# A chunked delta rule: new queue order for the halved chunks, and identity turns on TensorE at the change of state

## The chip, the cores and the metric

One core of one Trainium2 chip runs the whole program. The metric is device time in microseconds (us) of that core, the median of the runs shown.

## The reference, cut to what matters

The program is two layers of attention, scans and experts over x of 4 x 256 x 256. The change lies in one of its eight parts, a gated delta rule with 16 heads of 128 in each of 4 sequences, so 64 lanes of a 128 x 128 state:

```python
def step(S, t):
    q_t, k_t, v_t, a_t, b_t = t
    y = jnp.einsum('bhvk,bhk->bhv', S, k_t)
    err = y - v_t
    S = a_t[..., None] * S - (b_t[..., None] * err)[..., None] * k_t[:, :, None, :]
    o = jnp.einsum('bhvk,bhk->bhv', S, q_t)
    return (S, o)
```

After the scan come a layer norm over each head, a gate sigmoid(x Wg), and the product with Wo.

## The kernel before, in words

The 256 time steps are four blocks of 64. In each block `heads_and_norm` makes q, k, v and the decays a, while the block before is normed and projected. A block has two groups of 32 steps (o = 0 and 1), and a group has four chunks of 8 (jj = 0 to 3; ci = 4 o + jj). At the start of a group the state S of all 64 lanes is turned and multiplied with the keys and queries (`state_t`, `columns`), which gives F, the share of the old state. Between the two groups stands the change of state: the errors W are turned (`turn`), `update` multiplies them with the keys, VectorE adds this to S (`add_update`), and S is turned again for the next group.

Within a chunk VectorE (DVE) runs `chunk`: `key_decays` multiplies the chunk's key products M with decays; `base` puts the starting errors into PSUM; a chunk is solved in two halves of 4 steps, where the second needs products of the first (WH4, turned and multiplied on TensorE in `first_half`, taken in by `carry`). It then writes the errors, lane by lane decayed (WNS, or W in the last chunk), and makes the answers of the queries. TensorE (PE) carries the errors of all chunks so far to the next one: each `hop` turns 128 x 512 errors, ScalarE (ACT) copies them, and 16 small products follow. A chunk jj has jj + 1 hops, and the next chunk's `base` waits for the last of them. POOL (GpSimd) prepares decays for the chunk ahead (`prepare`), and masks the key products (`own_lanes`).

Each engine runs its list of instructions in the order in which the program writes it; the lists meet at semaphores. So the order of the lines is the order of the queues. Beside the chunk's own work, these lists hold `key_rows` (16 keys turned, 16 ACT copies), the decay of the 64 state lanes on ACT (L2589), and in group o = 1 the sixteen `gate` products of the layer's output gate (L2282, 4 per chunk) with their sigmoids.

The list of SP, which starts the transfers, matters too. M is loaded anew for every chunk (`spread`, L1920), into one of two rooms, so chunk ci can be asked for once chunk ci - 2 is finished. The gate's weights WG come four heads at a time (L1946). Both stand in one loop, which the change leaves as it is:

```python
for ci in range(2, NC):
    ...
    spread(n, ci)
    if ci >= NI:
        j = ci - NI
        sp.wait_ge(rest_mm, z["rest_mm"] + NI - 1)
        if j:
            sp.wait_ge(gate_mm, z["gate_mm"] + 4 * j)
        sp.dma_start(WG[:], ...).then_inc(wg_in, 16)
```

`gate_mm` counts finished gate products, `wg_in` the landed weights; `gate(n, h)` waits for load h // 4. `key_decays` of a chunk waits for its M (`m_in`).

Of the kernel before, what the change touches and what calls it, by code (L numbers as in the profile page):

```python
# [1678 lines left out]
def delta_attention(core):  # L1679
# [48 lines left out]
    ZB = sb("ZB", [P, 4 * QU], BF16)  # L1728
    AO = sb("AO", [P, BH])
# [39 lines left out]
    with nc.Block() as block:  # L1769
# [65 lines left out]
        def _(dve):  # L1835
# [24 lines left out]
            "f_d": NO * NS, "ds_d": NO, "dd_d": NC, "mk_d": NC, "mq_d": NC, "fp_d": NC, "wdec_d": NO * (NI - 1), "kt_mm": NO * NR,  # L1860
            "kr_d": NO * NR, "w_d": NC, "base_d": NC, "q_d": NC, "o_d": NC, "wt_mm": NR * NO, "wt_d": NR * NO,
            "kc_d": NO, "ch_mm": NO, "ch_d": NO, "cn_mm": NO, "cn_d": NO, "gh_d": NO, "gn_d": NO * (NI - 1), "wh_d": NC, "ht_mm": NC, "nh_d": NC,
# [21 lines left out]
    MB = flat_df[:, 0:4 * B * NI].rearrange("p (j i b) -> p j i b", j=NI, i=4)  # L1884
    MH = flat_df[:, 4 * B * NI:8 * B * NI].rearrange("p (j g l) -> p j g l", j=NI, g=2)
# [3 lines left out]
    with nc.Block() as block:  # L1889
# [74 lines left out]
        def _(pool):  # L1964
# [66 lines left out]
            def own_lanes(n, o):  # L2031
# [5 lines left out]
                c.then(nc.gpsimd.tensor_tensor(MB, SAME[:].unsqueeze(1).unsqueeze(1).broadcast_to([P, NI, 4, B]),  # L2037
# [6 lines left out]
                pool.wait_ge(cn_d, z["cn_d"] + o + 1)  # L2044
                for s in range(NI - 1):
                    x, w = BLOCKS.index((s, s + 1)), NI - 1 - s
                    g = GN[:, x:x + w].rearrange("p x (l w) -> p x l w", w=2 * C)
                    nc.gpsimd.tensor_tensor(g, g, MB[:, s].rearrange("p i b -> p (i b)").unsqueeze(1).unsqueeze(3)
                                            .broadcast_to([P, w, 4 * B, 2 * C]), ALU.mult).then_inc(gn_d, 1)

            def prepare(n, ci):
# [16 lines left out]
                q = M[:, r, :, 1]  # L2068
# [21 lines left out]
                nc.gpsimd.tensor_tensor(F[:, :, 0, cols], F[:, :, 0, cols], V[:, :, at:at + C], ALU.subtract).then_inc(fp_d, 1)  # L2090
                pool.wait_ge(m_in[r], 16 * (NC // 2 * n + ci // 2 + 1))
# [3 lines left out]
            for n in range(NBLK):  # L2095
# [4 lines left out]
                for ci in range(NC):  # L2100
# [9 lines left out]
                    else:  # L2110
# [4 lines left out]
                        pool.wait_ge(wdec_d, z["wdec_d"] + rests(o, jj))  # L2115
                    if ci + 1 < NC:
                        prepare(n, ci + 1)
            heads_and_norm(NBLK)

        @block.tensor  # L2120
        def _(pe):
# [67 lines left out]
            def key_products(n, o):  # L2189
# [18 lines left out]
                for x, (old, new) in enumerate(BLOCKS):  # L2208
                    cols = slice(new * C, (new + 1) * C)
                    bank, first = (1 + x, 0) if x < 4 else (6, (x - 4) * 4 * QU)  # L2210
# [9 lines left out]
            def first_half(n, ci):  # L2220
# [7 lines left out]
                pe.wait_ge(gh_d, z["gh_d"] + o + 1)  # L2228
                pe.wait_ge(nh_d, z["nh_d"] + ci + 1)
# [8 lines left out]
            def hop(n, o, jj, s):  # L2238
# [8 lines left out]
                pe.wait_ge(gn_d, z["gn_d"] + rests(o, s) + 1)  # L2247
                if s == 0 and not jj:
                    pe.wait_ge(res_d, z["res_d"] + NI * o + 1)
# [108 lines left out]
            for n in range(NBLK):  # L2358
# [569 lines left out]
```

## Time and profile before

| what | value |
|---|---|
| median of 3 runs | 2786.93 us (2782.4 to 2798.67) |
| the profiled execution: its own time / its span | 2790.64 us / 2788.7 us |
| busy share of the span: PE, DVE, ACT, POOL | 76%, 54%, 42%, 38% |
| mean granted clock of TensorE | 0.827 |
| the part with the delta rule | about 990 to 2477 us of the span |
| one block of 64 steps | about 356 us |
| group o = 0 of a block, first `key_decays` to the turn of the errors | 79 to 82 us |
| group o = 1, likewise | 88.6 to 92.4 us |

Times in the rows below are us from the start of the span. A row of the timeline has the start, the time that it took, the engine, the line of the kernel, the operation, what it writes and reads, and how many instructions were merged; in brackets stands how long the engine was idle before, and what released it.

### The profile page before, as it was taken

Reading aid. Unit: us, or ns where it says so; the run is one execution under the profiler, and the core shown is the slowest. Engines: PE = TensorE matmul, PEld = TensorE weight load, DVE = VectorE, ACT = ScalarE, POOL = GpSimd, SP = SyncE. Lnnn points to the kernel's source line nnn. Section 1 sums busy time; section 2 is a strip of 40 time slices with the busy share of each in tenths; the row PEclk is TensorE's granted clock in tenths of the full one; section 3 lists DMA queues with packets and bytes.
Section 4 is the critical chain, followed back from the end, with each engine's and each line's share of the span. In section 5 each row is a group of like instructions: output and inputs, shape, how many; then the busy total and the mean of one; then the engine's idle time right before and its main releaser. Section 6 shows DMA issues by size and latency. Waiting matters only on the chain. (4 is left out here: it accounts for less than half of the span.)

```text
span 2788.7 us, 45057 instructions
## 1 busy us (share of the span) xinstructions
PE 2106.8 (76%) x16812; PEld 1630.0 (58%) x16824; DVE 1504.5 (54%) x3258; ACT 1177.4 (42%) x2885; POOL 1062.2 (38%) x982
## 2 busy tenths in 40 slices
PE   8596549888879958576795667965779657668798
PEld 5364226566557847465675556854558546546586
DVE  2223632266663338646676566856568566446533
ACT  3112311145453328343564435644346444325433
POOL 0223022210006525837238471385713757110154
PEclk9698779989989979666896577976779758789899
DMA  8422022200015023211222112222122221120240
GB/s 276 122 25 50 0 90 23 37 20 22 1 41 185 0 50 98 71 47 61 84 73 78 46 62 69 84 63 65 61 69 84 63 65 54 38 55 2 86 140 15
DMA packets 138316, 179.45 MB, mean 64 GB/s; under 512 B 62048, under 2 KB 114544, under 8 KB 132992
## 3 DMA queue, kind: packets, MB, share of 16 engines
q1 hardware_dynamic: 129952, 166.46, 19.4%
q0 software_dynamic: 8160, 10.26, 2.3%
q8 instruction: 130, 2.13, 0.3%
q14 instruction: 74, 0.61, 0.1%
HBM read 154.52 MB, written 22.17 MB: 63 GB/s over the span
## 5 line engine op out<-in xcount | busy, mean ns | idle before, releaser
L2618 DVE SCALAR_TENSOR_TENSOR XT<-M_delta,CW_delta,XT 128x256 f32<-128x256 f32 x576 | 249.7, 494 | 79.3 <-ACT M_delta L2437 49.2
L2135 PE MATMUL PS<-XP_delta,X 128*128 128x268 f32 (+1 forms) x1024 | 242.1, 389 | 15.5 <-DMA X<-in_L_attn_b_heads 15.5
L2135 PEld LDWEIGHTS PS<-XP_delta,X 128*128 128x128 f32 x1024 | 192.7, 189 | 66.7 <-DMA X<-in_L_attn_b_heads 19.6
L1541 PE MATMUL PS<-XP_rffn,UW_rffn 128*128 128x512 f32 x816 | 194.8, 395 | 5.0 <-POOL UW_rffn L1495 4.6
L1541 PEld LDWEIGHTS PS<-XP_rffn,UW_rffn 128*128 128x128 f32 x816 | 155.7, 191 | 38.8 <-issue 6.3
L1273 ACT ACTIVATE PR_attn<-PS,NM_attn 128x256 f32<-128x256 f32 (+1 forms) x384 | 130.7, 448 | 103.7 <-DVE NM_attn L1343 103.7
L2254 PE MATMUL PS<-GN_delta,TR_delta 32*128 32x64 f32 x1536 | 94.3, 419 | 82.8 <-ACT TR_delta L2553 82.8
L1495 POOL TENSOR_TENSOR UW_rffn<-W_rffn,UW_rffn 128x512 fp32r<-128x512 f32 x34 | 44.2, 1301 | 295.1 <-ACT UW_rffn L1602 295.1
L561 POOL DMA_INDIRECT sums<-XS_moe,token_moe x46 | 71.7, 1559 | 220.9 <-ACT XS_moe L661 202.0
L2589 ACT ACTIVATE S_delta<-S_delta,AO_delta 128x128 f32<-128x128 f32 x512 | 153.0, 392 | 0.0
L2166 PE MATMUL PS<-KQ_delta,TR_delta 128*128 128x64 f32 x1024 | 138.8, 283 | 12.3 <-DVE TR_delta L2635 12.1
L2254 PEld LDWEIGHTS PS<-GN_delta,TR_delta 32*128 32x128 f32 x1536 | 86.7, 320 | 99.8 <-issue 99.8
L1663 DVE TENSOR_TENSOR SU_rffn<-PS,CB_rffn 128x512 f32<-128x512 f32 x68 | 47.0, 691 | 179.8 <-PE PS L1541 159.7
L2166 PEld LDWEIGHTS PS<-KQ_delta,TR_delta 128*128 128x128 f32 x1024 | 133.9, 204 | 16.5 <-DVE TR_delta L2635 16.5
L1504 POOL TENSOR_TENSOR HP_rffn<-HF_rffn,HP_rffn 128x512 fp32r<-128x512 f32 x68 | 92.0, 1373 | 115.6 <-ACT HP_rffn L1625 115.6
L1343 DVE TENSOR_REDUCE NM_attn<-PS 128x4 f32<-128x512 f32 (+1 forms) x144 | 94.8, 682 | 47.6 <-PE PS L1155 47.6
L1975 POOL TENSOR_SCALAR XT<-M_delta,CW_delta,CB_delta 128x256 f32<-128x256 f32 x64 | 51.0, 796 | 179.9 <-ACT M_delta L2437 179.9
L1613 ACT ACTIVATE SG_rffn<-PS 128x512 f32<-128x512 f32 x68 | 40.7, 598 | 156.9 <-PE PS L1541 156.9
L733 DVE COPY HT_moe<-PS 128x512 f32<-128x512 f32 x46 | 31.8, 691 | 134.7 <-PE PS L619 134.7
L2435 ACT ACTIVATE XT<-PS,CB_delta,CW_delta 128x256 f32<-128x256 f32 x128 | 72.3, 565 | 73.9 <-PE PS L2135 71.8
L1556 PE MATMUL PS<-HP_rffn,DW_rffn 128*128 128x512 f32 x408 | 99.8, 394 | 3.9 <-POOL DW_rffn L1506 3.9
L2650 DVE TENSOR_TENSOR PS<-PS,DC_delta 128x512 f32<-128x512 f32 x48 | 33.3, 694 | 125.1 <-PE PS L2254 115.5
(457 smaller groups left out, 5356.7 us busy)
## 6 DMA issues: line engine op xcount, KB each, us to landing
M_delta<-gram_delta SPq DMA_DIRECT2D x32, 1280.0 KB, 5.9
X<-in_L_attn_b_heads SPq DMA_DIRECT2D x64, 512.0 KB, 3.5
EW<-in_L_ffn_w SPq DMA_DIRECT2D x24, 512.0 KB, 10.2
CB_rffn<-routes_rffn SPq DMA_DIRECT2D x20, 512.0 KB, 21.9
XN<-in_L_attn_b_outs SPq DMA_DIRECT2D x16, 512.0 KB, 3.6
F_delta<-in_L_attn_b_outs SPq DMA_DIRECT2D x4, 2048.0 KB, 8.1
W_rffn<-in_L_ffn_tiles SPq DMA_DIRECT2D x4, 1536.0 KB, 11.0
slots<-pad SPq DMA_DIRECT2D x2, 2967.0 KB, 14.7
```

The source lines that it names most:

```text
L561: nc.gpsimd.indirect_dma_start(core.sums[:], bass.IndirectOffsetOnAxis(ap=token[:, t:t + 1], axis=0), XS[:, t, 0:D], None, compute_op=ALU. ...
L1273: last = nc.scalar.activation(PR[:, u % (2 * ROWS), j * w:(j + 1) * w], PS[:, r, j * w:(j + 1) * w], ACT.Exp, bias=NM[:, u % (2 * ROWS), j ...
L1343: nc.vector.tensor_reduce(NM[:, u % (2 * ROWS), 0:per], PS[:, r, :].rearrange("p (h j) -> p h j", h=per), AX.X, ALU.max, negate=True).then ...
L1504: nc.gpsimd.tensor_tensor(HP[1][:, r, x], HF[:, n, :], HP[0][:, r, x], ALU.subtract).then_inc(hl_d, 1)
L1541: last = nc.tensor.matmul(PS[:, 4 + 2 * n + q, :], UW[qw][:, r, (q * KD + k) * P:(q * KD + k + 1) * P], XP[qx][:, k, n * NB:(n + 1) * NB], ...
L1556: last = nc.tensor.matmul(PS[:, n * KD + q, :], DW[qw][:, r, q * P:(q + 1) * P], HP[qx][:, r, n * NB:(n + 1) * NB], start=start and step == 0,
L2135: last = nc.tensor.matmul(PS[:, 1 + i, 0:B * (WIN - halo)], WH[:, r, i, k, :], XP[:, k, :, n * BT + halo:n * BT + WIN], start=(k == 0), st ...
L2166: last = nc.tensor.matmul(PS[:, 5 * (g % 2), i * 2 * OC:(i + 1) * 2 * OC].rearrange("p (q t) -> p q t", q=2), TR[:, g % 3, i * P:(i + 1) * ...
L2254: last = nc.tensor.matmul(PS[:, 1 + k, at], NEW[rows, i], GN[rows, BLOCKS.index((s, jj + 1)), at], start=jj == 0, stop=jj == 0 or (s == jj ...
L2435: nc.scalar.activation(TMP[:, r, i], PS[:, 1 + i, 0:B * WIN].rearrange("p (b t) -> p b t", b=B)[:, :, TAPS - 1:], ACT.Identity, bias=CB[:, ...
L2589: last = nc.scalar.activation(S[:, lane, :], S[:, lane, :], ACT.Copy, scale=AO[:, lane:lane + 1])
L2618: nc.vector.scalar_tensor_tensor(TMP[:, r, i], RAW[:, r, i, :, tau:tau + BT], CW[:, i, h, tau:tau + 1], TMP[:, r, i], ALU.mult, ALU.add).t ...
```

## The change

- TensorE: in `key_products` only the products of the first pair of chunks are made ahead of the first chunk; the other five pairs (80 matmuls) follow the first chunk's half (`cross_products`). `key_rows` moves from chunk 0 to chunk 1, behind its hop. The gates no longer come four per chunk: 3, 2, 3 and 8, and all but two of them behind the chunk's last hop. In group o = 0 the identity is turned 20 times between the last chunk's errors and their turn; 20 more turns stand behind the first `update`.
- ACT: all hops of a chunk are copied before the state lanes are decayed; gates and decays are interleaved; lanes per chunk go from 10, 18, 18, 18 to 12, 12, 22, 18.
- DVE: the second `carry` comes ahead of the second solve, so that `res_d` is raised earlier. In chunk 0 `base` multiplies F with the decay itself, and subtracts V for the keys.
- POOL: no decay of F in chunk 0; the queries' decay waits until DVE has made `key_decays`; the masks MB get a tile of their own, and the other five pairs are masked after the next chunk's `prepare`.
- SP: nothing.

The diff, cut to its core (semaphore counts and copies of code that only moves are left out):

```diff
+    GATED = (3, 5, 8, H)
+    beside = lambda o, jj: (range(NR) if jj == 1 else (), range(GATED[jj - 1] if jj else 0, GATED[jj]) if o else ())
...
# POOL
                 if jj == 0:
                     decays(n, o)
+                    return
+                if jj == 1:
                     pool.wait_ge(f_d, z["f_d"] + NS * (o + 1))
...
+            def queries(n, ci):
+                z, r = base_of(n), ci % 2
+                pool.wait_ge(mk_d, z["mk_d"] + ci + 1)
...
+                    queries(n, ci)
                     if ci + 1 < NC:
                         prepare(n, ci + 1)
+                    if jj == 0:
+                        for s, (first, last) in enumerate(((1, 3), (3, 5), (5, 6))):
+                            cross_lanes(n, o, s, first, last)
...
# TensorE
                     key_products(n, o)
+                    cross_products(n, o, range(1))
                     for jj in range(NI):
                         ci = o * NI + jj
-                        gates = range(4 * jj, 4 * jj + 4) if o else ()
-                        if jj:
-                            for h in gates:
-                                gate(n, h)
-                            if o:
-                                pe.wait_ge(gate_d, z["gate_d"] + 4 * jj + 4)
+                        rows, gates = beside(o, jj)
                         first_half(n, ci)
                         if jj == 0:
-                            pe.wait_ge(cn_d, z["cn_d"] + o + 1)
-                            pe.wait_ge(f_d, z["f_d"] + NS * (o + 1))
-                            for r in range(NR):
-                                key_rows(n, o, r)
-                            pe.wait_ge(kr_d, z["kr_d"] + NR * (o + 1))
-                            for h in gates:
-                                gate(n, h)
-                            if o:
-                                pe.wait_ge(gate_d, z["gate_d"] + 4)
+                            pe.wait_ge(res_d, z["res_d"] + ci + 1)
+                            pe.wait_ge(cn_d, z["cn_d"] + 2 * o + 1)
+                            cross_products(n, o, range(1, HOPS))
+                            pe.wait_ge(cn_d, z["cn_d"] + 2 * o + 2)
                         elif jj < NI - 1:
...
                             for x in range(jj):
                                 hop(n, o, jj, x)
+                        else:
+                            for h in gates[:2]:
+                                gate(n, h)
+                            gates = gates[2:]
                         pe.wait_ge(w_d, z["w_d"] + ci + 1)
                         if jj + 1 < NI:
                             hop(n, o, jj, jj)
-                        else:
-                            pe.wait_ge(wdec_d, z["wdec_d"] + rests(o, jj))
-                            for r in range(NR):
-                                turn(n, o, r)
+                            pe.wait_ge(nw_d, z["nw_d"] + HOPS * o + hop_no(jj, jj) + 1)
+                        for r in rows:
+                            key_rows(n, o, r)
+                        if rows:
+                            pe.wait_ge(kr_d, z["kr_d"] + NR * (o + 1))
+                        for h in gates:
+                            gate(n, h)
+                        if o:
+                            pe.wait_ge(gate_d, z["gate_d"] + GATED[jj])
+                    if not o:
+                        for x in range(20):
+                            nc.tensor.transpose(PS[:, 6, 0:P], core.ident[:], core.ident[:])
+                    pe.wait_ge(wdec_d, z["wdec_d"] + rests(o, NI - 1))
+                    for r in range(NR):
+                        turn(n, o, r)
                     if o + 1 < NO:
                         for r in range(NR + 1):
                             if r < NR:
                                 update(n, o, r)
+                            if r == 0:
+                                pe.wait_ge(wt_d, z["wt_d"] + NR * (o + 1))
+                                for x in range(20):
+                                    nc.tensor.transpose(PS[:, 6, 0:P], core.ident[:], core.ident[:])
...
# ACT
-            cuts = [0, 10, 28, 46, BH]
+            cuts = [0, 12, 24, 46, BH]
...
                         if jj == 0:
-                            for r in range(NR):
-                                key_rows(n, o, r)
-                            if o:
-                                gates(n, jj)
+                            cross_products(n, o)
                             act.wait_ge(ds_d, z["ds_d"] + o + 1)
-                        elif jj < NI - 1:
-                            for x in range(jj):
+                        if jj < NI - 1:
+                            for x in range(jj + 1):
                                 hop(n, o, jj, x)
-                        for lane in range(cuts[jj], cuts[jj + 1]):
-                            last = nc.scalar.activation(S[:, lane, :], S[:, lane, :], ACT.Copy, scale=AO[:, lane:lane + 1])
-                        if jj < NI - 1:
-                            hop(n, o, jj, jj)
-                        else:
-                            last.then_inc(sdec_d, 1)
-                            for r in range(NR):
-                                turn(n, o, r)
+                        for r in rows:
+                            key_rows(n, o, r)
+                        at = cuts[jj]
+                        for h in gates:
+                            gate(n, h)
+                            then = min(at + 3, cuts[jj + 1] - 1)
+                            if then > at:
+                                decay_state(at, then)
+                            at = then
+                        last = decay_state(at, cuts[jj + 1])
...
# DVE
                 if jj == 0:
-                    return nc.vector.tensor_copy(out, F[:, :, q, cols])
+                    return nc.vector.tensor_tensor(out, F[:, :, q, cols], DC[:, r, :, q:q + C], ALU.mult)
...
                 c.then(base(o, jj, r, 0, FK))
+                if not jj:
+                    c.then(nc.vector.tensor_tensor(FK, FK, V[:, :, ci * C:(ci + 1) * C], ALU.subtract))
...
                 c.then(carry(r, 0))
+                carry(r, 1).then_inc(res_d, 1)
                 c.then(nc.vector.tensor_tensor(FK[:, :, HC:], FK[:, :, HC:], carried(0), ALU.add))
                 solve(k, 1)
...
-                carry(r, 1).then_inc(res_d, 1)
```

## Rows read from the trace of the kernel before

**Rows 1.** Timeline of DVE, block 1, group o = 0.
```profile
1484.32 2.52 DVE L2658 TENSOR_TENSOR M_delta<-M_delta,DD_delta 128x1264 f32<-128x1264 f32 x1
...
1495.70 0.49 DVE L2675 TENSOR_TENSOR TR_delta<-PS,DR_delta 128x128 f32<-128x128 f32 x2 [3.99 <-PE PS L2234]
...
1508.81 0.70 DVE L2650 TENSOR_TENSOR PS<-PS,DC_delta 128x512 f32<-128x512 f32 x1 [2.41 <-POOL F_delta L2090]
...
1530.20 0.70 DVE L2650 TENSOR_TENSOR PS<-PS,DC_delta 128x512 f32<-128x512 f32 x1 [2.24 <-PE PS L2254]
...
1536.85 0.49 DVE L2675 TENSOR_TENSOR TR_delta<-PS,DR_delta 128x128 f32<-128x128 f32 x2 [1.00 <-PE PS L2234]
...
1545.77 1.48 DVE L2658 TENSOR_TENSOR M_delta<-M_delta,DD_delta 128x1264 f32<-128x1264 f32 x1
...
1555.39 0.70 DVE L2650 TENSOR_TENSOR PS<-PS,DC_delta 128x512 f32<-128x512 f32 x1 [8.15 <-PE PS L2254]
...
1562.03 0.49 DVE L2675 TENSOR_TENSOR TR_delta<-PS,DR_delta 128x128 f32<-128x128 f32 x2 [1.02 <-PE PS L2234]
```

**Rows 2.** Timeline of PE, block 1: key products, hops, turns, key rows, gates.
```profile
1487.33 2.04 PE L2215 MATMUL PS<-KQ_delta,XT 128*32 128x64 f32 x128 [1.34 <-issue]
...
1547.56 1.98 PE L2254 MATMUL PS<-GN_delta,TR_delta 32*128 32x64 f32 x32 [0.77 <-ACT TR_delta L2553]
...
1553.28 1.98 PE L2254 MATMUL PS<-GN_delta,TR_delta 32*128 32x64 f32 x32 [2.70 <-ACT TR_delta L2553]
...
1565.90 3.76 PE L2186 MATMUL PS<-ident,XT 128*128 128x128 f32 x16 [4.00 <-DVE XT L2707]
...
1620.05 1.97 PE L2176 MATMUL PS<-ident,KQ_delta 128*128 128x128 f32 x8
...
1625.77 6.53 PE L2282 MATMUL PS<-XP_delta,XN 128*128 128x256 f32 x16 [1.23 <-ACT KQ_delta L2533]
...
1687.26 4.82 PE L2282 MATMUL PS<-XP_delta,XN 128*128 128x256 f32 x16
...
1699.90 3.59 PE L2186 MATMUL PS<-ident,XT 128*128 128x128 f32 x16 [3.98 <-DVE XT L2707]
```

**Rows 3.** Timeline of ACT, block 1: state lanes and copies.
```profile
1547.31 5.36 ACT L2589 ACTIVATE S_delta<-S_delta,AO_delta 128x128 f32<-128x128 f32 x18
...
1553.52 2.50 ACT L2574 COPY XT<-WNS_delta 128x128 f32<-128x128 f32 x12
```

**Rows 4.** Timeline of DVE, block 1, group o = 1.
```profile
1607.54 1.47 DVE L2658 TENSOR_TENSOR M_delta<-M_delta,DD_delta 128x1264 f32<-128x1264 f32 x1
...
1614.29 0.69 DVE L2649 COPY PS<-F_delta 128x512 f32<-128x512 f32 x1 [5.29 <-POOL F_delta L2090]
...
1638.36 0.70 DVE L2650 TENSOR_TENSOR PS<-PS,DC_delta 128x512 f32<-128x512 f32 x1 [7.04 <-PE PS L2254]
```

**Rows 5.** Timeline of SP, block 1, group o = 1.
```profile
1632.38 0.39 SPq L1946 DMA_DIRECT2D XN<-in_L_attn_b_outs  x1
1632.87 0.46 SPq L1920 DMA_DIRECT2D M_delta<-gram_delta  x1
```

**Rows 6.** Transfers issued from 1631 to 1634 us: KB each, us to landing.
```profile
M_delta<-gram_delta SPq DMA_DIRECT2D x1, 1280.0 KB, 7.0
XN<-in_L_attn_b_outs SPq DMA_DIRECT2D x1, 512.0 KB, 4.1
```

**Rows 7.** Timeline of DVE, changes of state in blocks 1 and 2.
```profile
1571.51 2.29 DVE L2744 TENSOR_TENSOR S_delta<-S_delta,PS 128x2048 f32<-128x2048 f32 x1 [0.59 <-PE PS L2271]
...
1929.05 2.29 DVE L2744 TENSOR_TENSOR S_delta<-S_delta,PS 128x2048 f32<-128x2048 f32 x1 [0.67 <-PE PS L2271]
...
1959.17 1.47 DVE L2658 TENSOR_TENSOR M_delta<-M_delta,DD_delta 128x1264 f32<-128x1264 f32 x1
```

**Rows 8.** Stretches: us, busy us (x) of PE, PEld, DVE, ACT, POOL, PEclk, DMA share, GB/s.
```profile
1580.00:1590.00 10.00, 10.00 (x72) 9.66 (x71) 2.69 (x2) 2.31 (x6) 0.00 (x0) 0.50 0.01 2
...
1936.00:1959.00 23.00, 20.45 (x227) 19.60 (x227) 9.20 (x10) 10.63 (x26) 0.00 (x0) 1.00 0.01 2
```

More of the change, by code:

```diff
@@ L2036, in own_lanes @@
                                         ALU.mult)
-                c.then(nc.gpsimd.tensor_tensor(MB, SAME[:].unsqueeze(1).unsqueeze(1).broadcast_to([P, NI, 4, B]),
+                c.then(nc.gpsimd.tensor_tensor(MB[:], SAME[:].unsqueeze(1).unsqueeze(1).broadcast_to([P, NI, 4, B]),
                                                BETAC[:, :, c0:c0 + NI].rearrange("p i c -> p c i").unsqueeze(3).broadcast_to([P, NI, 4, B]),
@@ L2043, in own_lanes, with cross_lanes @@
                                         ALU.mult).then_inc(gh_d, 1)
[L2044 to L2049, printed above, removed]
+                cross_lanes(n, o, 0, 0, 1)
+            def cross_lanes(n, o, s, first, last):
+                pool.wait_ge(cn_d, base_of(n)["cn_d"] + 2 * o + (2 if last > 1 else 1))
+                g = GN[:, first:last].rearrange("p x (l w) -> p x l w", w=2 * C)
+                nc.gpsimd.tensor_tensor(g, g, MB[:, s].rearrange("p i b -> p (i b)").unsqueeze(1).unsqueeze(3)
+                                        .broadcast_to([P, last - first, 4 * B, 2 * C]), ALU.mult).then_inc(gn_d, 1)
             def prepare(n, ci):
@@ L2207, in key_products, with cross_products @@
                 last.then_inc(ch_mm, 1)
-                for x, (old, new) in enumerate(BLOCKS):
+            def cross_products(n, o, blocks):
+                for x in blocks:
+                    old, new = BLOCKS[x]
                     cols = slice(new * C, (new + 1) * C)
-                    bank, first = (1 + x, 0) if x < 4 else (6, (x - 4) * 4 * QU)
+                    bank, first = (x, 0) if 0 < x < 5 else (6, x // 5 * 4 * QU)
                     for i in range(4):
@@ L2246, in hop @@
                 last.then_inc(nw_mm, 1)
-                pe.wait_ge(gn_d, z["gn_d"] + rests(o, s) + 1)
-                if s == 0 and not jj:
-                    pe.wait_ge(res_d, z["res_d"] + NI * o + 1)
+                pe.wait_ge(gn_d, z["gn_d"] + NI * o + (s + 2 if jj else 1))
                 pe.wait_ge(nw_d, x)
@@ L2544, in answer, with gate, decay_state @@
                 nc.scalar.copy(V[:, :, ci * C:(ci + 1) * C], PS[:, 5, :].rearrange("p (n t) -> p n t", t=C)).then_inc(o_d, 1)
-            def gates(n, jj):
-                for h in range(4 * jj, 4 * jj + 4):
-                    act.wait_ge(gate_mm, base_of(n)["gate_mm"] + h + 1)
-                    nc.scalar.activation(GATES[:, h // 2, h % 2], PS[:, 6 + h % 2, 0:B * BT], ACT.Sigmoid).then_inc(gate_d, 1)
+            def gate(n, h):
+                act.wait_ge(gate_mm, base_of(n)["gate_mm"] + h + 1)
+                nc.scalar.activation(GATES[:, h // 2, h % 2], PS[:, 6 + h % 2, 0:B * BT], ACT.Sigmoid).then_inc(gate_d, 1)
+            def decay_state(first, last):
+                for lane in range(first, last):
+                    done = nc.scalar.activation(S[:, lane, :], S[:, lane, :], ACT.Copy, scale=AO[:, lane:lane + 1])
+                return done
             def hop(n, o, jj, s):
@@ L2565, in _ @@
                         ci = o * NI + jj
+                        rows, gates = beside(o, jj)
                         if jj:
                             answer(n, ci - 1)
-                            if o:
-                                gates(n, jj)
                         if jj == NI - 1:
@@ L2579, in _ @@
                         if jj == 0:
-                            for r in range(NR):
-                                key_rows(n, o, r)
-                            if o:
-                                gates(n, jj)
+                            cross_products(n, o)
                             act.wait_ge(ds_d, z["ds_d"] + o + 1)
-                        elif jj < NI - 1:
-                            for x in range(jj):
+                        if jj < NI - 1:
+                            for x in range(jj + 1):
                                 hop(n, o, jj, x)
-                        for lane in range(cuts[jj], cuts[jj + 1]):
-                            last = nc.scalar.activation(S[:, lane, :], S[:, lane, :], ACT.Copy, scale=AO[:, lane:lane + 1])
-                        if jj < NI - 1:
-                            hop(n, o, jj, jj)
-                        else:
-                            last.then_inc(sdec_d, 1)
-                            for r in range(NR):
-                                turn(n, o, r)
+                        for r in rows:
[8 more added lines that the diff above has]
+                        last = decay_state(at, cuts[jj + 1])
+                    last.then_inc(sdec_d, 1)
+                    for r in range(NR):
+                        turn(n, o, r)
                     if o + 1 < NO:
```

29 lines of the change are left out of this document (18 added, 11 removed).

## The prediction, as it went on record before the changed kernel ran
> **What bounds the kernel now.** I first read the page: TensorE is busy for 76% of the span and no engine is full, so a sum of busy times says nothing here. The change lies in the delta rule's part, so I went to the timeline of VectorE there, which carries the chain of the errors from chunk to chunk, and at each bracket looked up who released it. Then I read TensorE, ScalarE and GpSimd between the same times, the granted clock by stretches, and, since gates move, the list of SP and the transfers.
>
> Call K the first `key_decays` of a group, B the start of a chunk's `base`, c the start of its first `carry`. Three things are to be seen. The chain is a loop through three engines: B to c is 6.65 us (1530.20 to 1536.85), c to the next `key_decays` 8.92, that op 1.5 [rows 1]. The next B then waits for the last hop, 8.15 us before chunk 3 [rows 1]. And that hop itself sat 2.70 us waiting for an ACT copy, against 0.77 for its neighbour: ACT was decaying 18 state lanes, 5.36 us [rows 2, 3]. A hop costs 5.72 - (2.70 - 0.77) = 3.8 us. In group 1 chunk 0 starts only 6.75 us after K, behind POOL's decay of F, and chunk 1 30.8 us after K, behind key rows and four gates [rows 2, 4].
>
> **Group o = 0.** *Chunk 0.* `base` no longer waits for POOL; it starts at K + 1.5 and has two ops, as in the other chunks, so c = K + 8.2, against K + 11.4 before [rows 1], where the half's turn stood behind 96 key products. From c: 1.0 for both carries, then the other 80 key products. 64 of them took 2.04 with 1.34 of issue idle ahead [rows 2], so 80 are between 2.6 (no idle) and 5.2 (two idles); I take 4.5, nearer to the row with its idle. Their copies are 1,280 columns at 2.50 per 1,536 [rows 3], 2.1. The hop to B is 1.9 for turn and copy and 2.1 from product to `base` (1553.28 to 1555.39). B1 = K + 19.8 against 24.5. *Chunk 1.* `res_d` comes 3 us earlier and no lane stands ahead of the copy, so hops end at c + 9.5 and DVE itself (8.92 + 1.5) is last: 17.1 against 21.4. *Chunk 2.* Here the moved work bites. Key rows now start when the hop ends, B1 + 16.1, and take 5.7 (1620.05 to 1625.77, [rows 2]); behind them on ACT are 12 lanes (0.298 each, 3.6) and the answer's copy (0.5), so the copy of the turned half comes at B1 + 25.9, where it is wanted 4.7 after B2, at B1 + 21.8: 4.1 late. The chunk is 6.65 + 4.1 + 1.9 + 3 x 3.8 + 0.1, 24.2 against 25.2. *Chunk 3.* Likewise 22 lanes (6.6), 0.5 and 2.5 of copies make it 2.6 late, and the earlier carry adds 0.5: 13.6 to the turn against 10.5. Sum 74.7, against 79.3, 81.6, 80.7 and 79.8 in the four blocks: -23 us.
>
> **Change of state.** The 20 identity turns stand behind the wait for the errors, so they are on the path: 16 turns are 3.76 at 1.2 GHz [rows 2], 20 are 4.7. In return the clock should be up for what follows. Before, add 0 started 5.6 us after the turn, and from it to K took 30.1 in block 2, which ran at 1.00 after 1936 us, but 36.0 in block 1, where TensorE was granted 0.50 with no idle at all [rows 7, 8]. New: 4.7, turn and update at the upper level 4.5 (my estimate, between 5.6 and its half), then 29.6 (block 2 less 0.5 for one update): 38.8, against 39.8, 41.6, 35.8 and 39.9. That is -2 us. The second 20 cost nothing at the upper level, for they take about 2.4 and TensorE waits 2.3 for the add anyway [rows 7]; at the lower level 2.4 of their 4.7 would show. If the clock stays low throughout, the four changes cost +28.
>
> **Group o = 1.** This decides. SP's list is untouched, and in it M of chunk 6 stands behind the weights for gates 4 to 7, which wait until gate 3 is done. Before, gate 3 was done in chunk 0: SP issued both at 1632.38 and 1632.87 [rows 5], before chunk 1's `base` even started (1638.36, [rows 4]), so nothing waited. Now gate 3 stands in chunk 1 (ci = 5), behind its last hop and behind the key rows. M of chunk 7 stands behind gate 7 in the same way, now behind chunk 6's hops. M can't be there before its chunk is due. Worked out from K:
> - `base` at K + 2.9 (between 1.5, no wait, and 6.75, as before; near the end of the last F product), c4 = K + 9.6, B1 + 11.6 later at K + 21.2, against 30.8. Gates 0 to 2 then stand in TensorE's and ACT's lists (1.6 each at the lower level): c5 1.7 late, K + 29.5.
> - hops end c5 + 9.5; key rows 5.7; gate 3 1.6 (6.53 / 4, [rows 2]); two issues 0.6; M lands in 7.0 with the weights ahead of it [rows 6]; `key_decays` 1.5: the next base is at K + 55.4. Hops alone would allow c5 + 10.5, K + 40.0: 15.4 lost.
> - c6 = K + 62.0; three hops end c6 + 13.3; gates 5 to 7 are 4.5 (four took 6.53 at the lower and 4.82 across a rise); 0.6, 7.0, 1.5: the last base at K + 89.0, 13.5 lost.
> - c7 = K + 95.6; errors ready 4.35 later, K + 100.0 (3.87 before from c to turn, [rows 1, 2], and 0.5 for the carry). Gates 10 and 11 follow, 3.3; only then are the weights of 12 to 15 asked for, 0.1 + 4.1 [rows 6]; four gates 4.8 to 6.5, I take 5.5; a sigmoid 0.5: the turn starts at K + 113.5, 13.5 after the errors, against 0.06.
>
> Before, K to turn was 92.4 (1607.54 to 1699.90), twice more about that, and 88.7 in block 3. New 4 x 113.5: +88 us.
>
> A rule of the Trainium skill bears on the last gates (TensorE: Matmul & The Clock Gate, "HAM oscillation"): a product loop that waits for a transfer before every short burst finds the array back at its lower clock. By it the gates behind the 4.1 us wait take 6.5 and not 5.5, and the sum is 4 us higher. It speaks against splitting these gates around a load; that rows 8 show 0.50 with TensorE full agrees that the level lags behind the work.
>
> A second rule (SBUF — State Buffer, "Who interferes with whom"): VectorE with two SBUF inputs and GpSimd lock each other out for a whole instruction. By it the new wait of the queries' decay spares `key_decays` the collision, since GpSimd then stands still. The rows agree that the op varies, 2.52 and 1.48 [rows 1]; with 2.52 in all 32 chunks the sum would be 33 higher, with 1.48 it stays.
>
> **The sum.** 2790.6 (the profiled execution) - 23 - 2 + 88 = 2854; it lay 3.7 above the median of its runs, so 2850. What differs by less than 0.5% (14 us) can hardly be told from no change.
>
> **Rivals.**
> - *The gates run at the upper clock.* For it: they are dense work, and key rows or hops run ahead of them. Against: the four behind the key rows took 6.53. Price per block: gate 3 -0.8, gates 5 to 7 -1.9, the end -3.1; 4 x 5.8 = -23: 2827.
> - *The fillers don't lift the clock.* For it: 0.50 under full load in rows 8. Against: it did rise within the turn and update in all four blocks. +28 in place of -2: 2880.
> - *Faster: SP's holds are not what ends last.* If M and the weights landed in time, 15.4 + 13.5 + 4.2 would go, but ACT's late copies and the gates in TensorE's list come up behind them (7 and 2.6): 23.5 per block, 94 in all: 2756, which is the reordering's worth by itself. For it: before, none of these waits shows. Against: the gate count is a plain semaphore wait ahead of M. It turns faster once the stalls that SP causes are under some 17 of these 33 us per block.
> - *M alone in time:* gate 4 still waits for its weights and holds the next half's turn, so 6.5 + 10.9 per block, 70 in all: 2780, no change to be told.
>
> **How the numbers follow.** Forecast as summed 0.58, its own range 2838 to 2864 (half an issue idle, one gate's level, M at 6 to 8 us in each block); upper clock 0.16; fillers fail 0.12; M alone in time 0.06; faster 0.08. The range goes from 2815 (upper clock, chunk 0 without issue idle) to 2880 and leaves out the last two and a margin. Slower 0.86, same 0.06, faster 0.08.
>
> **What would show it.** Right: `key_decays` of chunks 6 and 7 idle about 15 and 13 us, released by a transfer into M, itself issued just after gates 3 and 7; L2282 with an idle of some 4 us on the gate weights after the last errors; the turn 11 to 15 us after the errors; chunk 1 of group 0 near 17 us; `columns` at 1.00 in every block. Wrong: M issued ahead of gate 3, or group 1 below 100 us from K to turn. The forecast fails most easily if the chain between K and gate 3 is much shorter than summed, or if ACT's late copies are later than the transfers.

## The result, and the profile after

The changed kernel takes 2859.0 us (median of 4 runs, 2849.9 to 2868.5) against 2792.8 us of the kernel before, run beside it: ratio 1.0233, 95% interval 1.0169 to 1.0296. It is slower, by about 65 us. The profiled execution has a span of 2853.6 us (its own time 2855.6), 64.9 more than before, at a mean granted clock of 0.825.

The three parts of the prediction, read from the timelines of all four blocks as in the front (us; before in brackets):

| part | block 0 | 1 | 2 | 3 | sum | change | predicted |
|---|---|---|---|---|---|---|---|
| group o = 0, K to the end of chunk 3 | 74.5 (79.3) | 74.3 (81.6) | 74.4 (80.7) | 74.4 (79.8) | 297.6 | -23.8 | -23 |
| change of state, from there to K of o = 1 | 47.0 (39.8) | 39.5 (41.6) | 38.8 (35.8) | 38.7 (39.9) | 164.0 | +6.8 | -2 |
| group o = 1, K to the turn | 110.2 (92.4) | 117.2 (92.4) | 114.0 (92.4) | 113.5 (88.7) | 454.8 | +89.1 | +88 |

The three make +72.1; some 5 of the 7 us between that and the span are gained between the turn and the next block's K, 1.4 to 2.0 in each of three blocks.

The list of waits of block 1's group o = 1 (engine, what it does, what it waits for; us in total, times, longest) has a first row that before had nothing like:

```profile
DVE M_delta L2694 <- DMA M_delta<-gram_delta: 34.4, 2, 17.5
...
PE PS L2299 <- DMA XN<-in_L_attn_b_outs: 7.3, 2, 3.7
```

VectorE's timeline there. K is 1615.79, where it was 1607.54 in [rows 4]:

```profile
1615.79 1.47 DVE L2694 TENSOR_TENSOR M_delta<-M_delta,DD_delta 128x1264 f32<-128x1264 f32 x1
1618.72 0.70 DVE L2685 TENSOR_TENSOR PS<-F_delta,DC_delta 128x512 f32<-128x512 f32 x1 [1.47 <-ACT F_delta L2525]
...
1622.54 2.58 DVE L2685 TENSOR_TENSOR PS<-F_delta,DC_delta 128x512 f32<-128x512 f32 x1
...
1626.52 1.01 DVE L2711 TENSOR_TENSOR TR_delta<-PS,DR_delta 128x128 f32<-128x128 f32 x4 [0.65 <-PE PS L2253]
...
1636.77 0.70 DVE L2686 TENSOR_TENSOR PS<-PS,DC_delta 128x512 f32<-128x512 f32 x1
...
1644.63 0.70 DVE L2686 TENSOR_TENSOR PS<-PS,DC_delta 128x512 f32<-128x512 f32 x1 [3.96 <-ACT V_delta L2575]
...
1647.47 1.01 DVE L2711 TENSOR_TENSOR TR_delta<-PS,DR_delta 128x128 f32<-128x128 f32 x4 [0.89 <-PE PS L2253]
...
1673.04 1.48 DVE L2694 TENSOR_TENSOR M_delta<-M_delta,DD_delta 128x1264 f32<-128x1264 f32 x1 [16.84 <-DMA M_delta<-gram_delta]
...
1707.32 1.48 DVE L2694 TENSOR_TENSOR M_delta<-M_delta,DD_delta 128x1264 f32<-128x1264 f32 x1 [17.54 <-DMA M_delta<-gram_delta]
...
1718.85 0.69 DVE L2748 TENSOR_TENSOR XT<-PS,X 128x512 f32<-128x512 f32 x1
...
1736.70 2.29 DVE L2784 TENSOR_TENSOR S_delta<-S_delta,PS 128x2048 f32<-128x2048 f32 x1 [12.65 <-PE PS L2288]
```

`base` of chunk 1 starts at K + 21.0, where it started at K + 30.8: this part of the reordering gains 9.8 us. Then `key_decays` of chunk 6 sits 16.84 us on its transfer and that of chunk 7 17.54. SP's list says why (compare [rows 5], both issued in chunk 0):

```profile
1664.77 0.39 SPq L1948 DMA_DIRECT2D XN<-in_L_attn_b_outs  x1
1665.26 0.46 SPq L1922 DMA_DIRECT2D M_delta<-gram_delta  x1
1699.85 0.38 SPq L1948 DMA_DIRECT2D XN<-in_L_attn_b_outs  x1
1700.33 0.46 SPq L1922 DMA_DIRECT2D M_delta<-gram_delta  x1
1723.46 0.38 SPq L1948 DMA_DIRECT2D XN<-in_L_attn_b_outs  x1
```

and TensorE's timeline shows the gates (L2299) whose end each of these issues follows:

```profile
1662.62 2.07 PE L2299 MATMUL PS<-XP_delta,XN 128*128 128x256 f32 x4 [1.23 <-ACT KQ_delta L2564]
1668.26 2.08 PE L2299 MATMUL PS<-XP_delta,XN 128*128 128x256 f32 x4 [3.57 <-DMA XN<-in_L_attn_b_outs]
...
1694.29 5.49 PE L2299 MATMUL PS<-XP_delta,XN 128*128 128x256 f32 x12
...
1719.60 3.78 PE L2299 MATMUL PS<-XP_delta,XN 128*128 128x256 f32 x8 [0.67 <-DVE XT L2748]
1727.12 5.36 PE L2299 MATMUL PS<-XP_delta,XN 128*128 128x256 f32 x16 [3.74 <-DMA XN<-in_L_attn_b_outs]
```

Gate 3 ends at 1664.7 and the weights and M go out; gates 5 to 7 end at 1699.8 and the next pair goes out; the last weights hold gates 12 to 15, and with them the turn, which starts 13.4 us after the errors (written from 1718.85 to 1719.54).

### The profile page after: what moved, and what is told of

It reads as the page before. It is cut to its first block and busy times, and to the rows that moved or that the text cites. A ratio compares the mean times of both kernels' runs of the same rounds, so it can differ in the third digit from the quotient of the medians.

```text
span 2853.6 us, 45401 instructions
## 1 busy us (share of the span) xinstructions
PE 2141.2 (75%) x16984; PEld 1655.2 (58%) x16984; DVE 1510.2 (53%) x3266; ACT 1175.9 (41%) x2893; POOL 1035.0 (36%) x966
## 5 line engine op out<-in xcount | busy, mean ns | idle before, releaser
L2180 PE MATMUL PS<-KQ_delta,TR_delta 128*128 128x64 f32 x1024 | 139.9, 285 | 16.8 <-DVE TR_delta L2671 16.7
L2180 PEld LDWEIGHTS PS<-KQ_delta,TR_delta 128*128 128x128 f32 x1024 | 135.3, 206 | 20.6 <-DVE TR_delta L2671 20.6
L2243 PE MATMUL PS<-ident,TR_delta 128*128 128x128 f32 x64 | 18.4, 384 | 153.1 <-DVE TR_delta L2732 151.7
L2299 PE MATMUL PS<-XP_delta,XN 128*128 128x256 f32 x256 | 99.2, 557 | 38.6 <-DMA XN<-in_L_attn_b_outs 30.7
L2694 DVE TENSOR_TENSOR M_delta<-M_delta,DD_delta 128x1264 f32<-128x1264 f32 x32 | 48.7, 1522 | 132.0 <-DMA M_delta<-gram_delta 130.5
L2102 POOL TENSOR_TENSOR M_delta<-M_delta,DD_delta 128x1280 f32<-128x1280 f32 x32 | 93.1, 2910 | 68.1 <-DVE M_delta L2694 66.6
L2784 DVE TENSOR_TENSOR S_delta<-S_delta,PS 128x2048 f32<-128x2048 f32 x28 | 64.1, 2288 | 96.0 <-PE PS L2288 96.0
```

Of the source, the lines that this page charges most:

```text
L2102: nc.gpsimd.tensor_tensor(q, q, by_h(DD[:]), ALU.mult).then_inc(mq_d, 1)
L2180: last = nc.tensor.matmul(PS[:, 5 * (g % 2), i * 2 * OC:(i + 1) * 2 * OC].rearrange("p (q t) -> p q t", q=2), TR[:, g % 3, i * P:(i + 1) * ...
L2299: last = nc.tensor.matmul(PS[:, 6 + h % 2, 0:B * BT], WG[:, h % 4, k * P:(k + 1) * P], XP[:, k, :, n * BT + TAPS - 1:n * BT + WIN], start= ...
```

## The experiments

Each kernel ran beside the kernel before on the same chip; ratios are to it, with a 95% interval, and the changed kernel stands at 1.0233. Sums over the four blocks run from a group's K to the errors (T), and from T to the next K, in the profiled execution: before 320.8, 157.8 and 365.1 us (group 0, change of state, group 1); changed 297.0, 164.6 and 405.5, where group 1 then has its late turn still ahead. That lateness is read as T to the first add: 5.2 us before, 15.6 to 17.3 changed. A difference taken against 1.0233 carries that ratio's own interval, some 18 us either way.

**1. M asked for ahead of the weights.** Same transfers and waits, but SP asks for M of chunk ci + 1 before it waits for the gates.

```diff
-                for ci in range(2, NC):
+                for ci in range(2, NC + 1):
...
+                    if ci < NC:
+                        spread(n, ci)
+                    if ci == NI + 1:
+                        continue
...
-                        j = ci - NI
+                        j = ci - NI - (ci > NI)
```

> The changed kernel with one edit in SP's list: M of chunks 6 and 7 is asked for ahead of the gate weights that wait for gates 3 and 7. My theory (SP's held transfers of M are what ends last): the 16 us idles ahead of key_decays of chunks 6 and 7 go, but the time doesn't fall by their whole sum of 33 per block, since gate 4 still waits for its weights in TensorE's list and holds the next half's turn, and ACT's lanes and copies come behind gates 5 to 7. From the changed kernel's durations in block 1: c6 at K + 58 instead of 65, c7 at K + 86 instead of 99.6, the turn at K + 104 instead of 117; four blocks -53, so about 2805, 0.5% above the kernel before. Rival A (M is hidden behind the gates anyway): within 10 us of 2859. Rival B (M was all of it): -130, about 2730.

2824.9 us, ratio 1.0146 (1.0108 to 1.0184): 24 us back by the ratios, 34 by the medians, not 54. The waits on M are gone and group 1 falls from 405.5 to 367.3, but another comes up, and the turn stays late (T to the first add 16.9 to 17.6). VectorE's timeline in block 1:

```profile
1661.99 0.70 DVE L2689 TENSOR_TENSOR PS<-PS,DC_delta 128x512 f32<-128x512 f32 x1 [12.83 <-ACT V_delta L2578]
```

and TensorE's, the gate that this copy waits behind:

```profile
1656.38 2.07 PE L2302 MATMUL PS<-XP_delta,XN 128*128 128x256 f32 x4 [4.08 <-DMA XN<-in_L_attn_b_outs]
```

ScalarE's list has gate 4's sigmoid, and nine state lanes of 2.72 us together, ahead of the copy of the answers that the second half of `base` needs. The gate waits for weights that SP asked for only when gate 3 was done. So the two things that SP holds back cover one another: M alone is worth less than its wait shows.

**2. Four gates per chunk.** The only edit; no load is asked for late then.

```diff
-    GATED = (3, 5, 8, H)
+    GATED = (4, 8, 12, H)
```

> The changed kernel with one number set changed: gates 4, 4, 4, 4 per chunk in place of 3, 2, 3, 8, at the places of the new order; SP's list as it is. My theory: gate 3 is done in chunk 0 again, so M of chunk 6 is asked for a chunk earlier, M of chunk 7 behind gate 7, just in time, and no gate waits for weights; what stays is TensorE's list, key rows and four gates (12.8 us) between a hop and the next half's turn. The turn at K + 97 instead of K + 117: four blocks -80, 2780, about 0.5% below the kernel before. Rival (the loss comes from gates and key rows standing behind the hops, not from SP): no gain or a loss against 2859, since more gates stand behind the hops of chunks 4 to 6.

2786.9 us, ratio 0.9993 (0.9972 to 1.0014), 7 us over the expectation. With this edit alone the whole loss is gone. Why it isn't a gain has three parts: the identity turns are still there (experiment 5), T to the first add in group 1 is 9.8 us where it was 5.2, and VectorE waits for the same copy behind the gates:

```profile
1627.23 0.70 DVE L2686 TENSOR_TENSOR PS<-PS,DC_delta 128x512 f32<-128x512 f32 x1 [4.22 <-ACT V_delta L2575]
...
1653.76 0.70 DVE L2686 TENSOR_TENSOR PS<-PS,DC_delta 128x512 f32<-128x512 f32 x1 [9.59 <-ACT V_delta L2575]
...
1681.16 0.70 DVE L2686 TENSOR_TENSOR PS<-PS,DC_delta 128x512 f32<-128x512 f32 x1 [7.24 <-ACT V_delta L2575]
```

**3. Two rooms for the weights.** Gates stay at 3, 2, 3 and 8, and load j waits for the gates of load j - 2 and not j - 1; each room has a count of its own. Load 1 waits for the block's last scatter, which frees the second room; in block 1 it goes out at 1562.63, long before its gates.

```diff
-    WG = GR[:, 0].rearrange("p h w -> p (h w)").rearrange("p (r n) -> p r n", r=4)
+    WG = [GR[:, x].rearrange("p h w -> p (h w)").rearrange("p (r n) -> p r n", r=4) for x in range(2)]
...
-                        if j:
-                            sp.wait_ge(gate_mm, z["gate_mm"] + 4 * j)
+                        if j == 1:
+                            sp.wait_ge(sc_out[NC - 1], 16 * C * (n + 1))
+                        elif j:
+                            sp.wait_ge(gate_mm, z["gate_mm"] + 4 * (j - 1))
```

> The changed kernel with gates 3, 2, 3, 8 kept, fillers kept, and two rooms for the gate weights, so that load j waits only for the gates of load j - 2: SP no longer holds M of chunks 6 and 7, nor the weights of gates 4 and 12, while every list of the compute engines stays as changed. If SP's waits alone are the cause, group 1 falls from 117 to about 96 us in block 1 (hops, key rows and gates at the changed kernel's durations): -84, 2775. Rival (the new places of gates cost most of it, whatever SP does): above 2820, as with M ahead alone (2825).

2785.1 us, ratio 0.9981 (0.9954 to 1.0007). This takes away SP's holds and leaves all else of the change: 0.0252 of 2791, 70 us, is what they cost. The prediction's rival put both at 94; in block 1, 8.05 and 6.41 us of waits for the answers' copy come up in their place, where it had reckoned 7 and 2.6 for copies and gates.

**4. The identity turns, alone and apart.** Four kernels: the changed one without both sets of 20 (a), the changed one without the set ahead of the errors' turn (b), the kernel before with both sets (c), and the kernel before with only the set behind the update (d).

The set ahead, left out in a and b, added in c:

```diff
-                    if not o:
-                        for x in range(20):
-                            nc.tensor.transpose(PS[:, 6, 0:P], core.ident[:], core.ident[:])
```

The set behind, left out in a, added in c and d:

```diff
+                            if r == 0:
+                                pe.wait_ge(wt_d, z["wt_d"] + NR * (o + 1))
+                                for x in range(20):
+                                    nc.tensor.transpose(PS[:, 6, 0:P], core.ident[:], core.ident[:])
```

(a) 

> The changed kernel without both sets of 20 identity turns. The recorded forecast had them gain 2 us in all; in the changed kernel's trace the four changes of state, from the errors to K, sum to 164 us against 157 before, 8 of them from block 0, where the clock fell back. If the fillers are worth nothing: 2852 (-7). If the clock then stays low as before but the rest is as recorded: 2850 to 2862, not to be told from the changed kernel.

(b) 

> The changed kernel without the 20 identity turns ahead of the errors' turn; the 20 behind the first update stay. Theory (the set ahead stands on the path and costs its 4.4 to 4.7 us per block, the set behind costs the rest): of the 20 us that both sets cost in the changed kernel (2859 against 2839) about 15 come back with the first set gone, so near 2843. Rival (the set behind costs most, because it holds the second update up at the lower level): near 2855. Rival (the set ahead only moves where the clock falls, so that without it nothing is gained): 2859.

(c) 

> The kernel before with both sets of 20 identity turns and nothing else. Recorded forecast: -2 us, not to be told from the kernel before; errors to add 0 grows from 5.7 to about 9.2 in every block, add 0 to K falls to 29.6 in each. Rival (the fillers don't hold the clock): +7 to +28, a ratio of 1.003 to 1.01.

(d) 

> The kernel before with only the 20 identity turns behind the first update. Theory (the set ahead of the turn is what costs; the set behind is hidden behind the wait for VectorE's add and shortens the next two adds): the four changes of state fall from 157.8 to about 150, so -7 us, ratio near 0.9975. Rival (both sets cost, as the two together added 18 us): about +8.

| kernel | sets | us | ratio | four changes of state | T to add 0 |
|---|---|---|---|---|---|
| changed | both | 2859.0 | 1.0233 (1.0169 to 1.0296) | 164.6 | 7.7 to 8.2 |
| a | none | 2838.6 | 1.0190 (1.0150 to 1.0229) | 156.6 | 5.1 to 5.5 |
| b | behind | 2829.2 | 1.0148 (1.0126 to 1.0170) | 149.6 | 5.5 to 5.9 |
| before | none | 2786.9 | 1 | 157.8 | 5.8 to 6.1 |
| c | both | 2803.8 | 1.0064 (1.0039 to 1.0088) | 175.7 | 8.2 to 9.1 |
| d | behind | 2780.3 | 0.9967 (0.9946 to 0.9988) | 152.3 | 5.4 to 6.5 |

The intervals of c and d lie clear of one another, and that of d lies below 1. Those of b and the changed kernel meet at their ends (1.0170 and 1.0169); those of a and the changed kernel, and of a and b, overlap. The set ahead costs about 24 us in the changed kernel (0.0085; 30 by the medians) and 27 in the kernel before (0.0097). The set behind gains 9 us in the kernel before; the 12 in the changed one are not told from nothing by the times, but its changes of state fall by 7.0. TensorE's timeline with both sets in the changed kernel, block 1:

```profile
1576.30 4.33 PE L2427 MATMUL PS<-ident 128*128 128x128 f32 x20 [4.39 <-DVE XT L2748]
1580.46 1.04 PE L2200 MATMUL PS<-ident,XT 128*128 128x128 f32 x8
1581.74 1.15 PE L2200 MATMUL PS<-ident,XT 128*128 128x128 f32 x8 [0.24 <-ACT KQ_delta L2570]
1582.82 1.17 PE L2288 MATMUL PS<-KQ_delta 32*128 32x128 f32 x32
1583.92 2.40 PE L2438 MATMUL PS<-ident 128*128 128x128 f32 x20
1586.59 1.17 PE L2288 MATMUL PS<-KQ_delta 32*128 32x128 f32 x32 [0.27 <-DVE S_delta L2784]
...
1601.63 1.81 PE L2180 MATMUL PS<-KQ_delta,TR_delta 128*128 128x64 f32 x8
1603.37 2.09 PE L2288 MATMUL PS<-KQ_delta 32*128 32x128 f32 x32
```

and with the set behind alone (b), block 1:

```profile
1562.63 3.76 PE L2200 MATMUL PS<-ident,XT 128*128 128x128 f32 x16 [4.39 <-DVE XT L2745]
1566.33 1.62 PE L2288 MATMUL PS<-KQ_delta 32*128 32x128 f32 x32
1567.88 2.41 PE L2435 MATMUL PS<-ident 128*128 128x128 f32 x20
1570.56 1.17 PE L2288 MATMUL PS<-KQ_delta 32*128 32x128 f32 x32 [0.27 <-DVE S_delta L2781]
```

The first set holds the turn back by 4.16 us (1576.30 to 1580.46). For it, turn and update run at the upper level and are through 3.53 us after the turn's start, against 5.32: 1.8 back, a loss of 2.4 on the path and about 10 in four blocks. The four changes of state differ by more, 15.0 between the changed kernel and b and 23.4 between c and d, and the rest there is the clock: with both sets the products of block 1 are back at their slower times within the same stage (8 products of L2180 in 1.81 us, the update in 2.09), and the four adds lie 3.67, 7.78 and 9.93 apart; with the set behind alone 3.66, 7.79 and 7.79. The blocks differ: in block 0 of the changed kernel adds 1 and 2 lie 11.91 apart, in blocks 2 and 3 7.79. Kernel c has 11.33 to 11.90 there in every block, as three of the kernel before have, and d in two. What decides in which block the level falls is not shown. The profiled executions of the changed kernel and b differ by 29.7 us, so half of that lies outside the changes of state, 4.0 of it in group 1. The set behind is done 0.27 us before the next update is released by add 0, so it costs nothing.

**5. Four gates and no identity turns.** Do the parts add up? The edit of experiment 2, and both sets of experiment 4 left out:

```diff
-    GATED = (3, 5, 8, H)
+    GATED = (4, 8, 12, H)
```

> Gates 4, 4, 4, 4 and no identity turns: the two undone together. After the first runs my theory is that the loss has two separate parts, SP's held transfers with the gates' weights (72 us, measured by the four gates alone) and the fillers (some 20 us, measured twice), and that the rest of the new order is a gain. If they add up: 2787 - 18 = 2769, a ratio to the kernel before of 0.993. Rival (the fillers' price is only that of a changed kernel's luck with the clock): 2780 to 2790, ratio 0.996 to 1.0.

2768.3 us, ratio 0.9924 (0.9898 to 0.9950). As expected (2769): they add.

**6. Fewer state lanes ahead of copies that are waited for.** On top of experiment 5:

```diff
-            cuts = [0, 12, 24, 46, BH]
+            CUTS = ([0, 23, 25, 41, BH], [0, 13, 26, 38, BH])
```

> As the last one, and ACT's state lanes are spread anew: 23, 2, 16, 23 in group 0 and 13, 13, 12, 26 in group 1, in place of 12, 12, 22, 18. Theory (the prediction's: lanes behind key rows and hops make ACT's copy for the next half late, by 4.1 in chunk 2 and 2.6 in chunk 3; the trace shows VectorE waiting 3.40 for the answer's copy, then 1.08): group 0 falls from 74.4 to 70 us, group 1 by 3 to 4, about 2737 in all. Rival (VectorE or TensorE is right behind ACT): less than 10 us.

2763.8 us, ratio 0.9912 (0.9876 to 0.9949), 27 us short of the theory; by the times it is not told from experiment 5, and the rival's "less than 10 us" stands. Group 0 does fall, to 281.5 (70.2 to 70.5 per block, 70 expected) and group 1 from 356.9 to 344.7. But T to the first add of group 1, 9.9 before this edit, is now 12.5 to 14.0: the 26 lanes of chunk 7 stand ahead of the turn's copies on ScalarE. Even so, from the first K to the last errors the profiled execution is 24.4 us shorter than that of experiment 5; 5.6 of them go before the first K and 10.8 behind the last errors, where no edit was made. In the 40 us behind the last errors TensorE was granted 0.70, and 0.83 in experiment 5; why is open.

**7. Two rooms, no identity turns, lanes by group** (23, 2, 16, 23 and 12, 8, 12, 32), gates 3, 2, 3 and 8; then the same with group 1's lanes 20, 10, 14, 20; then the first again with the set of identity turns behind the update.

> Two rooms, gates 3, 2, 3, 8, no fillers, lanes 23, 2, 16, 23 and 12, 8, 12, 32. Sum of the single effects: 2775 - 18 - 4 x 7.5 = 2727, ratio 0.978, if they add up; above 2750 if they hide each other.

> Two rooms for the gate's weights, no identity turns, group 0 lanes 23, 2, 16, 23 as before, but in group 1 20, 10, 14 and 20 lanes for chunks 4 to 7 in place of 12, 8, 12 and 32. Theory (the 32 lanes of chunk 7 stand ahead of the turn's copies on ScalarE and make the turn's first add 15.3 us late, where 10 would do; twelve lanes fewer are 3.6 us per block): 2754.75 less 4 x 3.6, about 2741. Rival (what the earlier chunks get on top holds up a hop's copy there, as much as is saved): no change, 2755.

> Two rooms for the gate's weights, the lane cuts of the run before it (23, 2, 16, 23 and 12, 8, 12, 32), no identity turns ahead of the errors' turn, and the 20 identity turns behind the first update. Theory (the set behind the update fills a wait and keeps TensorE at the upper level, which made the four changes of state 149.6 us together in the changed kernel against 156.6 without any fillers): 7 to 10 us under the version without it, 2755, so near 2747. Rival (the difference of the two earlier runs was the runs' spread): 2755, no change.

| kernel | us | ratio | group 1, K to T | T to add 0 |
|---|---|---|---|---|
| lanes 12, 8, 12, 32 | 2754.8 | 0.9883 (0.9845 to 0.9921) | 329.1 | 15.3 |
| lanes 20, 10, 14, 20 | 2758.3 | 0.9895 (0.9866 to 0.9925) | 347.7 | 10.6 to 12.2 |
| the first, and the set behind | 2749.8 | 0.9856 (0.9827 to 0.9884) | 337.8 | 15.3 |

ScalarE's timeline of the first, block 1, shows lanes ahead of the turn's copies:

```profile
1676.20 3.32 ACT L2579 ACTIVATE S_delta<-S_delta,AO_delta 128x128 f32<-128x128 f32 x11
1679.41 1.06 ACT L2566 COPY KQ_delta<-PS 128x512 f32<-128x512 f32 x2
```

Moving twelve of them forward takes 3 to 5 us off T to the add and puts 4.6 on K to T: the rival was right, twelve lanes cost as much in the earlier chunks. All three stay above what was expected of them (2727, 2741, 2747), the first by 28, the last by 3. The last kernel has the lowest ratio, 1.4% under the kernel before; it changes the state in 145.4 us where the first takes 153.4. But the intervals of the two overlap, and its trace gives the 8.0 back in group 1 (337.8 against 329.1), so that it is the faster of the two is not shown.

## Why the prediction was right, and where it was off

The forecast was 2850 us, and 2859 was measured. By its steps:

- **Group o = 0**: -23 predicted, -23.8 measured. In block 1: B1 at K + 19.1 (19.8 predicted), then chunks of 18.7 (17.1) and 23.6 (24.2), and 12.9 to the end of chunk 3 (13.6). The sum is nearer than its terms: one that is 1.6 over, with a wait of 1.16 us for POOL in it, is made up by three that are 0.6 or 0.7 under. The late copies of chunk 2 are there, but by another path than predicted. The answers' copy holds the second half of `base`, for 3.40 us, and `carry` starts 10.15 us after B2 where 6.65 was free of waits: 3.5 late (4.1 predicted, for the copy of the turned half).
- **Group o = 1**: +88 predicted, +89.1 measured. Block 1 against the working from K: c4 10.7 (9.6), B1 21.0 (21.2), c5 31.7 (29.5), B2 58.6 (55.4), c6 65.3 (62.0), B3 92.9 (89.0), c7 99.6 (95.6), the turn 117.2 (113.5). The causal step, M and the weights behind the gate count in SP's list, is shown by experiments 2 and 3: take the late gates away or give the load a second room, and 67 to 70 us go. M alone is worth less than predicted: 24 to 34 us in experiment 1, where the rival "M alone in time" had 70. The losses measured against the hops are 1674.43 less (1647.47 + 10.5), 16.5, and 1708.71 less (1681.06 + 13.4), 14.3; predicted 15.4 and 13.5.
- **The late turn**: predicted 13.5 us behind the errors; 13.4 in block 1, 11.6 to 12.1 in the other three, where gates 10 and 11 took 1.99 us and not 3.78. Gates 12 to 15 behind their weights took 5.36, and 5.17 to 5.41 in the others, between the two levels as taken (5.5). By the rule of the Trainium skill (TensorE: Matmul & The Clock Gate, "HAM oscillation") a burst behind such a wait starts at the lower clock. The trace agrees, the gates of block 1 begin at 0.50; but the level rises before they are through (columns as in [rows 8]):

```profile
1727.10:1728.10 1.00, 0.98 (x2) 0.83 (x3) 0.00 (x0) 0.00 (x0) 0.00 (x0) 0.50 1.04 342
...
1731.10:1732.40 1.30, 1.30 (x7) 0.85 (x5) 0.00 (x0) 0.94 (x4) 0.00 (x0) 1.00 1.13 362
```

  So the 6.5 that the prediction made of the rule, the lower level throughout, was too long in all four blocks. Experiment 1 has it in two of its four, 6.55 behind a wait of 3.92 us in block 1.
- **Missed, small**: in chunk 0 the first `carry` of group 1 comes at K + 10.7 and not 9.6, since the new product of F took 2.58 us beside POOL (last section). Further, the second half of `base` waits for ScalarE's copy of the answers, 3.96 us in block 1's chunk 5, and makes c5 2.2 late. The prediction counted gates and lanes ahead of the copy into TR, and missed that the copy into V behind them holds `base` itself. Small here, it is VectorE's longest wait in block 1's group 1 in experiments 1 to 3: 12.83, 9.59 and 8.05 us.
- **Wrong: the change of state.** -2 predicted, +6.8 measured; by experiment 4 the two sets together cost about 12 us in the changed kernel (20 by the medians) and 18 in the kernel before. The step that failed is "in return the clock should be up for what follows": it took block 2 of the kernel before, granted 1.00 after 1936 us, as what the fillers give, 29.6 us from add 0 to K. Measured were 39.0, 31.6, 31.1 and 31.1. Three blocks still come out near the 38.8 predicted for the whole (39.5, 38.8, 38.7), which is luck: T to add 0 took 7.7 to 8.2 where 9.2 was reckoned. The level did rise within the first set, as forecast, but the products of block 1 were slow again some 20 us after it, those of block 0 10 us after, and in kernel c 10 to 11 us after. Block 0, which alone lost 8 us against the forecast, by stretches (columns as in [rows 8]):

```profile
1208.30:1218.30 10.00, 7.76 (x109) 6.60 (x107) 5.08 (x4) 3.22 (x6) 9.55 (x8) 1.00 0.39 133
1218.30:1228.00 9.70, 9.45 (x67) 9.11 (x68) 1.37 (x3) 2.31 (x6) 3.63 (x9) 0.51 0.00 0
1228.00:1238.00 10.00, 8.59 (x95) 7.92 (x93) 5.79 (x5) 5.32 (x13) 0.00 (x0) 0.96 0.01 2
1238.00:1252.00 14.00, 13.76 (x70) 13.76 (x71) 3.28 (x5) 3.21 (x9) 0.00 (x0) 0.53 0.00 0
```

  The rival that the fillers fail had the right sign, with 28 where 7 came. The claim that the second 20 cost nothing holds: they gain 9 us in the kernel before.
- **Not in the forecast**: the 5 us gained between the turn and the next block's K. They make up for part of the 9 that the change of state missed, so part of the nearness of 2850 to 2859 is luck.

The rival "faster: SP's holds are not what ends last" put the time without them at 2756, 94 us less. Experiment 3 is that case and took 2785: its price was some 24 us too high, and its condition, that the holds don't end last, was false.

## What to carry to other kernels

Before work is moved in one queue, look up which lists wait on its counts, the list that starts transfers first: everything behind such a wait, here an unrelated load, becomes as late as the work. When two loads are held by one wait, removing one shows little, so price them together. Filler products belong where the engine waits anyway; ahead of work that is waited for they cost here more than the higher level gave back.

## What the runs showed of the hardware

- The granted level didn't stay up for having been lifted early. In windows of the changed kernel (columns as in [rows 8]), the stretch right after the fillers of blocks 1 and 2 is not at 1.00 throughout, although TensorE is busy 28.5 of 32 or 33 us:

```profile
1584.00:1616.00 32.00, 28.50 (x290) 26.94 (x291) 14.53 (x13) 11.38 (x27) 10.06 (x12) 0.89 0.06 23
...
1955.00:1988.00 33.00, 28.47 (x326) 26.86 (x325) 14.77 (x13) 12.69 (x31) 11.43 (x13) 0.95 0.10 34
```

- `key_decays`, two SBUF inputs, fell from a mean of 1.966 us to 1.522 once POOL's multiplication of the queries' half waited for it, 14 us over 32 chunks; no run changes this wait alone. The collision seems to have moved: the new product of F with the decay, PSUM out of two SBUF inputs, takes 0.70 us alone, and 2.58 where POOL runs its M product. Groups by form for VectorE (count, busy, mean ns, idle before), and POOL's timeline beside the slow one at 1622.54:

```profile
L2694 DVE TENSOR_TENSOR M_delta<-M_delta,DD_delta 128x1264 f32<-128x1264 f32 x32 | 48.7, 1522 | 132.0 <-DMA M_delta<-gram_delta 130.5
L2685 DVE TENSOR_TENSOR PS<-F_delta,DC_delta 128x512 f32<-128x512 f32 x16 | 24.9, 1556 | 7.4 <-ACT F_delta L2525 7.4
```

```profile
1621.64 2.91 POOL L2102 TENSOR_TENSOR M_delta<-M_delta,DD_delta 128x1280 f32<-128x1280 f32 x1
```

The op on VectorE ends at 1625.12, some 0.6 us after POOL's at 1624.55, less than the 0.70 that it takes alone. By the Trainium skill (SBUF — State Buffer, "Who interferes with whom") a VectorE op with two SBUF inputs contends with a GpSimd op that reads SBUF, for a pair of ports that only one of them can hold. The trace agrees that such an op is held up beside POOL, here by 1.9 us; held until POOL's end it would have ended 0.1 us later than shown. The prediction priced two ends for `key_decays`, 33 us apart over 32 chunks, and took the lower, which held; the F product it had left out, 24.9 against 11.2 at 0.70 each.
